# A new order of work on all engines in the time-mixing layer, reciprocals of products of two halves, crossed numerators and one first norm for two sequences on GpSimd

## The chip, the cores and the metric

One Trainium2 chip, one core of it. The metric is the device time of one execution of the kernel in microseconds (us); lower is better. The core has five engines with queues of their own, each strictly in order: TensorE (PE in the profile), VectorE (DVE), ScalarE (ACT), GpSimd (POOL) and SyncE (SP, which issues most transfers). They wait for each other by semaphores.

## The reference, cut to what matters

The model has two layers. The first is RWKV time and channel mixing followed by a routed feed-forward of eight experts, the second is linear attention followed by soft-routed experts. All is float32. The change lies in the first half of layer 0, over 16 sequences of 256 tokens with 128 features:

```python
h = ln(x, ln1); h1 = time_shift(h)                 # first norm
k, v, r = mix(h, h1) @ (Wk, Wv, Wr)
wkv = (sum_{i<t} e^{(t-1-i)w + k_i} v_i + e^{u+k_t} v_t) / (sum_{i<t} e^{(t-1-i)w + k_i} + e^{u+k_t})
x = x + (sigmoid(r) * wkv) @ Wo                    # time mixing
h = ln(x, ln2); h1 = time_shift(h)                 # second norm
x = x + sigmoid(mix(h, h1) @ cm_Wr) * (relu(mix(h, h1) @ cm_Wk)**2 @ cm_Wv)   # channel mixing
x = layernorm(x_in + x)                            # third norm; then logits = x @ router_w, top-1 expert
```

The numerator and the denominator of wkv come from one scan over time, divided per column (token) and row (feature).

## The kernel before, in words

Features lie on the 128 partitions when a stage runs along time, tokens when a norm or an output is formed. Two sequences (u = 0 and 1) make a turn; there are eight turns. Four parts of the work are pipelined over turns, and one step runs them for four different turns: **N** (first norm of turn s+2, turned to columns), **M** (time mixing of turn s+1), **C** (channel mixing of turn s), **R** (third norm's columns, router logits, places and the scatter of rows into expert order, turn s-1). Steps go from s = -2 to 8: N, NM, NMC, then NMCR in s = 1 to 5 (s = 2 to 5 are a hardware loop), MCR, CR, R. After them come a routing table, the experts and layer 1, which the change leaves as they are.

Nothing but the written order of each engine's queue and its semaphore waits sets the order of a step. The queues before:

- PE: `mixed_columns` of keys and values of both sequences (L670-675), time receptance and the turn of the second norm for each (L676-684), the turn of the third norm and the first two channel keys for each (L685-694), router logits, channel receptance `receptance` (L636) and the last two keys for each (L703-707), `time_mixing_out(0)` (L626), channel values of both (L717), turns of the first norm (L721-726), `ranks`, `time_mixing_out(1)`.
- ACT: columns of the second norm and the tanh of r for both; `shares(0)` (L755: four relus and three exponentials); the third norm of sequence 1 (`normalise`, L743-752), then columns of the third norm of both (L802); `relus` and `squares` of the keys (L776-785) around `shares(1)`; the gates (L818); the first norm of both (L822) and its columns (L826); third norm of sequence 0, second norm of both.
- DVE: `exponents` of both (a running maximum and a difference, L983), statistics of the first norm, then `weighted_values` (L1089): `take_values`, `run_state` (the scan over 512 columns, numerator and denominator), `kept_part`, `both_parts`, `inverse` (a reciprocal of the 256 denominators, L1022), `receive` (times 1 + tanh), `mixed_values` (times the reciprocal; gives `y_cols`), with the router's small steps between; then the sums and statistics of the other norms (`first_sum`, `gate_values`, `second_sum`, `stats`, `spread`).
- POOL: `to_rstd` (L867: two small operations, a power -0.5, a product) once per norm and sequence, six a step; `x01` (L929: the sum of input and first output, which also allows the next load of `x_res`); `find_places`; `scatter` (four indirect transfers).
- SP: loads of `x_in_rows` behind the first norm, of `x_res` behind `x01`, copies of the third norm to `xa` and to `stage`; the copy to `stage` waits until the scatter before has landed.

In PE's queue the turn of the third norm of a sequence comes before its first keys:

```python
for u in range(U):                                   # L685
    if "R" in parts:
        pe.wait_ge(R["normed3_ready"][u], r * NT + NT)
        turn(bank(u, 2), normed3[u], R["turned3"][u])
    if "C" in parts:
        pe.wait_ge(R["h2_ready"][u], c + 1)
        ...
```

Of the kernel before, what the change touches and what calls it, by code (L numbers as in the profile page):

```python
# [73 lines left out]
def two_layer_kernel(nc, x_in, vecs_in, rows_in, consts_in, w, out):  # L74
# [26 lines left out]
    with ctx:  # L101
# [31 lines left out]
        eps = sb("eps", [P, 3, NT])  # L133
# [75 lines left out]
        def bufs(name, shape, dt=F32, scope=rw):  # L209
# [7 lines left out]
                 for k in (1, 2, 3)}  # L217
        moments = {k: bufs(f"moments_{k}", [P, NT, 6]) for k in (1, 2, 3)}
        normed1 = bufs("normed1", [P, NT, D])
# [16 lines left out]
        recip = bufs("recip", [P, T])  # L236
# [67 lines left out]


# [243 lines left out]
        with nc.Block() as block:  # L549
# [64 lines left out]
            def _(pe):  # L614
# [10 lines left out]
                def step(parts, n, m, c, r):  # L625
                    def time_mixing_out(u):  # L626
# [20 lines left out]
                    def ranks():  # L647
                        pe.wait_ge(chosen_ready, r + 1)
                        at = T + 2 * NT * E

                        def dst(first):
                            return bank(1, 0, at + first * E, at + (TURN_TILES + 1) * E)
# [17 lines left out]
                    if "M" in parts:  # L670
                        for u in range(U):
                            pe.wait_ge(R["h1_ready"][u], m + 1)
                            mixed_columns(bank(u, 1, 0, T), h1_cols[u], "tm_Wk", 0, D)
                            mixed_columns(bank(u, 1, T, 2 * T), h1_cols[u], "tm_Wv", 0, D
                                          ).then_inc(R["kv_ready"][u], 1)
                    for u in range(U):  # L676
                        if "M" in parts:
                            if "C" in parts and follows(c):
                                pe.wait_ge(R["rc_done"][u], c)
                            mixed_columns(bank(u, 3, 0, T), h1_cols[u], "tm_Wr", 0, D  # L680
                                          ).then_inc(R["r_ready"][u], 1)
                        if "C" in parts:
                            pe.wait_ge(R["normed2_ready"][u], c * NT + NT)
                            turn(bank(u, 0), normed2[u], R["turned2"][u])
                    for u in range(U):  # L685
                        if "R" in parts:
                            pe.wait_ge(R["normed3_ready"][u], r * NT + NT)
                            turn(bank(u, 2), normed3[u], R["turned3"][u])
                        if "C" in parts:
                            pe.wait_ge(R["h2_ready"][u], c + 1)  # L690
                            if "M" in parts:
                                pe.wait_ge(R["r_done"][u], m + 1)
                            for k in (0, 1):
                                channel_keys(u, k, bank(u, 3, k * T, (k + 1) * T))
                    if "R" in parts:
                        for u in range(U):
                            pe.wait_ge(R["xa_cols_ready"][u], r + 1)
                            for j in range(NT):
                                last = pe.matmul(bank(u, 0, T + j * E, T + (j + 1) * E),
                                                 xa_cols[u][:, j * P:(j + 1) * P], router_w[:, :],  # L700
                                                 start=True, stop=True)
                            last.then_inc(R["logits_ready"][u], 1)
                    if "C" in parts:  # L703
                        for u in range(U):
                            receptance(u)
                            for k in (2, 3):
                                channel_keys(u, k, bank(u, 2, (k - 2) * T, (k - 1) * T))
# [1187 lines left out]
```

## Time and profile before

| | |
|---|---|
| median of 3 runs | 717.41 us (715.91 to 718.39) |
| the profiled execution | 714.66 us, span 713.0 us |
| busy over the span | PE 633.4 us (89%), DVE 470.3 (66%), ACT 366.8 (51%), POOL 272.0 (38%) |
| mean granted clock of TensorE | 0.957 of full speed |
| instructions | 14,924 |

The steps of layer 0 fill the first 231 us of the span, the experts and layer 1 the rest. A busy time counts instructions between their start and their end; matmul ends are modelled and overlap, so the distance between two starts says more about PE. A number in brackets in a timeline row is the engine's idle time before the instruction, and what ended it.

### The profile page before, as it was taken

The page shows a single profiled execution, that of the slowest core. Times are in us where ns is not written, and L with a number is a line of the kernel's source. Part 1 is how long each engine was busy: PE and PEld are TensorE (multiplying, and loading weights), DVE is VectorE, ACT ScalarE, POOL GpSimd, SP SyncE. Part 2 cuts the span into 40 slices and gives each one's busy share as a digit, 9 for nine tenths or more (in the row PEclk, how much of TensorE's full clock was granted, in tenths as well). Part 3 has the DMA queues.
Part 4 walks back from the last instruction along what each step waited for, and adds up shares of the span by engine and source line. Part 5 has one row for each costly group of instructions (what it writes and reads, how often), then busy time and mean ns, then how long its engine had stood idle before and what let it go on. Part 6 is the DMA issues. An engine that isn't in the chain of part 4 may idle for free.

```text
span 713.0 us, 14924 instructions
## 1 busy us (share of the span) xinstructions
PE 633.4 (89%) x4107; PEld 522.3 (73%) x4108; DVE 470.3 (66%) x1518; ACT 366.8 (51%) x818; POOL 272.0 (38%) x574
## 2 busy tenths in 40 slices
PE   4498898889875399999988999999999999999995
PEld 3387797779764299999934678777777777877773
DVE  4888888889733355545425677778777777777742
ACT  3477768777734244454401455455554555545542
POOL 2315556756365421112044333344433443332201
PEclk9699999999987599999999999999999999999998
DMA  5081111111101577777400000000000000000000
GB/s 144 15 245 54 42 48 59 59 52 37 60 31 44 184 238 253 225 244 227 125 23 12 4 5 17 16 15 15 15 15 15 15 7 8 15 16 8 8 9 15
DMA packets 39458, 46.99 MB, mean 66 GB/s; under 512 B 5184, under 2 KB 31104, under 8 KB 39424
## 3 DMA queue, kind: packets, MB, share of 16 engines
q1 hardware_dynamic: 35520, 39.50, 18.0%
q0 software_dynamic: 3328, 6.82, 3.1%
q8 instruction: 15, 0.25, 0.1%
q10 hardware_dynamic: 576, 0.26, 0.1%
q14 instruction: 19, 0.16, 0.1%
HBM read 34.58 MB, written 7.80 MB: 59 GB/s over the span
## 4 chain that ended last, share of the span: by engine, by line
PE 38%; DVE 8%; issue 2%; POOL 1%; ACT 1%; DMA 0%; DVEq 0%; POOLq 0%; ACTq 0%
PE banks L1401 8%; PE banks L1407 5%; PE banks L1523 5%; PE banks L1536 4%; PE banks L1435 4%; PE banks L1421 3%; DVE token_peak L1782 2%; PE banks L1383 2%; PE banks L1467 1%; PE banks L1501 1%; PE banks L1529 1%; PE banks L1457 1%; DVE moments_e L1690 1%; PE banks L1427 1%; DVE summed_e L1775 1%
## 5 line engine op out<-in xcount | busy, mean ns | idle before, releaser
L439 PE MATMUL banks<-xg_cols,w 128*128 128x128 f32 x624 | 77.8, 279 | 0.0
L439 PEld LDWEIGHTS banks<-xg_cols,w 128*128 128x128 f32 x624 | 74.4, 196 | 0.2 <-issue 0.2
L497 DVE SCALAR_TENSOR_TENSOR hidden<-banks,b_cols,gate 128x128 f32<-128x128 f32 x156 | 43.9, 344 | 46.4 <-ACT gate L466 46.4
L466 ACT ACTIVATE gate<-banks,b_cols 128x128 f32<-128x128 f32 x156 | 44.5, 368 | 54.9 <-PE banks L439 54.9
L1407 PE MATMUL banks<-ffn_w,act_cols 128*128 128x128 f32 x512 | 66.2, 278 | 0.7 <-ACT act_cols L1558 0.7
L1407 PEld LDWEIGHTS banks<-ffn_w,act_cols 128*128 128x128 f32 x512 | 60.6, 192 | 7.9 <-issue 6.4
L1401 PE MATMUL banks<-slots_cols,ffn_w 128*128 128x512 f32 x128 | 64.1, 606 | 0.8 <-ACT slots_cols L1573 0.8
L1558 ACT ACTIVATE act_cols<-banks 128x512 f32<-128x512 f32 x64 | 38.2, 597 | 27.3 <-PE banks L1401 27.3
L523 POOL DMA_DIRECT2D xg<-sorted_x x40 | 21.9, 547 | 79.3 <-PE banks L448 61.0
L617 PE MATMUL banks<-consts,normed 128*128 128x128 f32 x96 | 18.9, 308 | 31.7 <-ACT normed L750 31.6
L1624 POOL TENSOR_TENSOR rstd_b<-mean_var_b,eps 128x2 f32<-128x2 f32 x16 | 3.1, 195 | 106.2 <-DVE mean_var_b L1693 106.2
L871 POOL TENSOR_TENSOR rstd<-mean_var,eps 128x2 f32<-128x2 f32 x48 | 11.5, 240 | 82.7 <-DVE mean_var L981 82.5
L429 PE MATMUL banks<-w,hidden 128*128 x312 | 41.3, 275 | 0.5 <-DVE hidden L497 0.5
L622 PE MATMUL banks<-h_cols,cm_Wk_now 128*128 128x256 f32 x128 | 41.1, 405 | 0.2 <-ACT r_tanh L794 0.2
L623 PE MATMUL banks<-h_cols,cm_Wk_before 128*128 128x256 f32 x128 | 40.0, 395 | 0.0
L617 PEld LDWEIGHTS banks<-consts,normed 128*128 128x128 f32 x96 | 12.5, 155 | 37.2 <-ACT normed L750 28.4
L910 POOL DMA_INDIRECT sorted_x<-stage,slot_now x32 | 33.4, 1043 | 16.7 <-issue 12.7
L429 PEld LDWEIGHTS banks<-w,hidden 128*128 128x128 f32 x312 | 37.9, 192 | 0.7 <-issue 0.7
L1597 ACT ACTIVATE combine<-banks 128x1024 f32<-128x1024 f32 x16 | 16.4, 1023 | 40.8 <-PE banks L1529 40.8
L874 POOL TENSOR_TENSOR rstd<-rstd,neg_half 128x2 f32<-128x2 f32 x48 | 35.6, 741 | 4.0
L1613 POOL DMA_INDIRECT y_got<-sorted_y,y_idx x32 | 32.5, 1015 | 9.3 <-issue 7.5
L1523 PE MATMUL banks<-xn,dispatch 128*128 128x129 f32 x256 | 34.2, 288 | 0.2 <-ACT dispatch L1589 0.2
(242 smaller groups left out, 1628.4 us busy)
## 6 DMA issues: line engine op xcount, KB each, us to landing
w<-w_dram SPq DMA_DIRECT2D x39, 512.0 KB, 4.5
xg<-sorted_x POOLq DMA_DIRECT2D x40, 64.0 KB, 4.0
sorted_y<-y_rows SPq DMA_DIRECT2D x39, 64.0 KB, 3.4
x_in_rows<-x_dram SPq DMA_DIRECT2D x16, 128.0 KB, 2.3
x_res<-x_dram SPq DMA_DIRECT2D x16, 128.0 KB, 2.2
xa<-normed SPq DMA_DIRECT2D x16, 128.0 KB, 2.1
stage<-normed SPq DMA_DIRECT2D x16, 128.0 KB, 2.1
out_dram<-final SPq DMA_DIRECT2D x16, 128.0 KB, 1.8
```

What stands on the lines that cost most here:

```text
L429: last = pe.matmul(dst, hidden[u][:, c, :], w2[:, bass.ds(e2, 1), c, :].squeeze(1), start=(c == 0), stop=(c == XC - 1))
L439: last = pe.matmul(bank(u, k, c * P, (c + 1) * P), w1[parity][u][:, lo:lo + P], xg_cols[u][:, :], start=True, stop=True)
L466: act.activation(gate[u][:, c, :], bank(u, 2, c * P, (c + 1) * P), ACT.Sigmoid, bias=b1_cols[:, bass.ds(e1 * GC + XC + c, 1)]).then_inc(ga ...
L497: last = dve.scalar_tensor_tensor(hidden[u][:, c, :], bank(u, 1, c * P, (c + 1) * P), b1_cols[:, bass.ds(e1 * GC + c, 1)], gate[u][:, c, : ...
L622: pe.matmul(dst, now[:, lo:hi], h[:, 1:T + 1], start=True, stop=False)
L623: return pe.matmul(dst, before[:, lo:hi], h[:, 0:T], start=False, stop=True)
L874: p.step(pool.tensor_tensor(rstd[u][:, :], rstd[u][:, :], neg_half[:, 0:NT], ALU.pow))
L910: pool.indirect_dma_start(sorted_x, bass.IndirectOffsetOnAxis(ap=slot_now[:, t:t + 1], axis=0), stage[u][:, j, :], None).then_inc(scattere ...
L1401: pe.matmul(banks[:, 6 + c % 2, :], ffn_w1[:, c * P:(c + 1) * P], slots_cols[ub][:, :], start=True, stop=True).then_inc(S["hid_ready"][ub], 1)
L1407: last = pe.matmul(banks[:, 6, s * D:(s + 1) * D], act_cols[ub][:, c, s * P:(s + 1) * P], ffn_w2[:, c, :], start=(c == 0), stop=(c == HC - 1))
L1523: last = pe.matmul(dst, dispatch[uf][:, j, s * P:(s + 1) * P], xn[uf][:, j, :], start=(j == 0), stop=(j == NT - 1))
L1558: act.activation(act_cols[ub][:, c, :], banks[:, 6 + c % 2, :], ACT.Gelu).then_inc(S["gelu_ready"][ub], 1)
```

## The change

1. **Reciprocals.** The 256 denominators a sequence are split into two halves of 128. DVE multiplies the halves (`multiplied`, 128 x 128) and takes the reciprocal of the product (128 x 128 instead of 128 x 256). 1/a is then b/(ab): GpSimd multiplies each numerator by the other half's denominator (`cross`), DVE's `receive` takes that in place of the numerator, and `mixed_values` multiplies both halves by the same reciprocal.
2. **First norm.** One `norm_scales` on GpSimd for the four tiles of both sequences replaces two `to_rstd` on two tiles each; ACT's `normalise(1, ...)` of both sequences waits for it.
3. **Order.** PE, ACT, DVE and POOL get a new written order of a step. `shares` becomes `shares_taken` and `shares_kept`; `scatter` works per sequence; `find_places` stands before the third norm of sequence 1; `x01` stands behind the first half of the scatter.
4. **A new place for the ranks.** Their PSUM columns move to bank (1, 3), so `ranks` waits for the channel gate of sequence 1, and time receptance of sequence 1 waits for `places`.

```diff
@@ TensorE, one step (the functions hold the matmuls that stood in the loops)
+                    def time_receptance(u):
+                        if "C" in parts and follows(c):
+                            pe.wait_ge(R["rc_done"][u], c)
+                        if u == 1 and "R" in parts and follows(r):
+                            pe.wait_ge(places_ready, r)
+                        mixed_columns(bank(u, 3, 0, T), h1_cols[u], "tm_Wr", 0, D).then_inc(R["r_ready"][u], 1)
...
+                    def turn_first(u):
+                        pe.wait_ge(R["normed1_ready"][u], n * NT + 2 * NT)
...
                     def ranks():
                         pe.wait_ge(chosen_ready, r + 1)
+                        pe.wait_ge(R["rc_done"][1], c + 1 if "C" in parts else r + 1)
...
+                        keys_and_values(0)
+                        time_receptance(0)
+                        turn_second(0)
+                        keys_and_values(1)
+                        turn_third(0)
+                        time_receptance(1)
+                        turn_second(1)
+                        first_keys(0)
+                        token_logits(0)
+                        first_keys(1)
+                        other_keys(0)
+                        turn_third(1)
+                        receptance(0)
+                        token_logits(1)
+                        other_keys(1)
+                        channel_values(0)
+                        turn_first(0)
+                        receptance(1)
                         time_mixing_out(0)
+                        channel_values(1)
+                        time_mixing_out(1)
+                        turn_first(1)
                         ranks()
@@ ScalarE, one step
+                        second_columns(0)
+                        time_gate(0)
+                        shares_taken(0)
+                        third_columns(0)
+                        shares_kept(0)
+                        time_gate(1)
+                        second_columns(1)
+                        relus(0, 0)
+                        shares_taken(1)
                         normalise(3, r, 1, gated, normed3)
+                        shares_kept(1)
+                        third_columns(1)
                         relus(1, 0)
                         relus(0, 1)
                         squares(0, 0)
                         squares(0, 1)
+                        squares(1, 0)
                         relus(1, 1)
+                        normalise(1, n, 0, x_in_rows, normed1)
+                        channel_gate(0)
+                        normalise(1, n, 1, x_in_rows, normed1)
                         squares(1, 1)
+                        first_columns(0)
+                        channel_gate(1)
                         normalise(3, c, 0, gated, normed3)
+                        first_columns(1)
                             normalise(2, m, u, x1, normed2)
@@ GpSimd
+                    def cross(u):
+                        pool.wait_ge(vec_m, m * VALUE_STEPS + BOTH_STEP[u])
+                        p2.step(pool.tensor_tensor(in_halves(crossed[u][:, :]), in_halves(frac[u][:, 0, :]),
+                                                   in_halves(frac[u][:, 1, :])[:, ::-1, :], ALU.mult))
+                    if "M" in parts:
+                        cross(0)
                     if "N" in parts:
                         for u in range(U):
-                            to_rstd(p1, 1, EPS_TM, n, u)
+                            pool.wait_ge(R["var1"][u], n * NT + NT)
+                        norm_scales(p1, both_mean_var[:, :, :, :].rearrange("p u j k -> p (u j) k"),
...
+                        cross(1)
                         to_rstd(p3, 3, EPS_LN, c, 0)
                             to_rstd(p2, 2, EPS_TM, m, u)
+                        find_places()
                         to_rstd(p3, 3, EPS_LN, c, 1)
+                        scatter(0)
...
+                        scatter(1)
@@ VectorE
-                def inverse(q, u, both):
+                def multiplied(q, u, both):
                     q.wait(both)
-                    return q.step(dve.reciprocal(recip[u][:, :], frac[u][:, 1, :]))
+                    return q.step(dve.tensor_tensor(product[u][:, :], frac[u][:, 1, 0:T // 2],
+                                                    frac[u][:, 1, T // 2:T], ALU.mult))
+                def inverse(q, u, product_run):
+                    q.wait(product_run)
+                    return q.step(dve.reciprocal(recip[u][:, :], product[u][:, :]))
                 def receive(q, m, u):
                     dve.wait_ge(R["r_done"][u], m + 1)
+                    dve.wait_ge(pool_rwkv[2], m * (POOL_VALUES + 3 * U) + u + 1)
+                    return q.step(dve.scalar_tensor_tensor(crossed[u][:, :], r_tanh[u][:, :], 1.0,
+                                                           crossed[u][:, :], ALU.add, ALU.mult))
...
+                        highest0 = highest(qm, m, 0)
+                        exponents(qm, 0, highest0)
+                        taken0 = stats(qn, 1, x_in_rows, 0)
+                        highest1 = highest(qm, m, 1)
+                        taken1 = stats(qn, 1, x_in_rows, 1)
+                        take_values(m, 0)
+                        spread(qn, 1, 0, taken0)
+                        exponents(qm, 1, highest1)
+                        state0 = run_state(qm, m, 0)
+                        spread(qn, 1, 1, taken1)
+                        kept0 = kept_part(qm, m, 0, state0)
+                        both0 = both_parts(qm, 0, kept0)
+                        take_values(m, 1)
+                        multiplied0 = multiplied(qm, 0, both0)
+                        inverse(qm, 0, multiplied0)
+                        state1 = run_state(qm, m, 1)
+                        save_logits(qr, r)
+                        received0 = receive(qm, m, 0)
+                        best_logit(qr)
+                        kept1 = kept_part(qm, m, 1, state1)
+                        candidates(qr)
+                        both1 = both_parts(qm, 1, kept1)
+                        preferences(qr)
+                        multiplied1 = multiplied(qm, 1, both1)
+                        mixed_values(qm, 0, received0)
+                        inverse(qm, 1, multiplied1)
+                        gated0 = second_sum(qc, c, 0)
+                        received1 = receive(qm, m, 1)
+                        spread(qc, 3, 0, gated0)
+                        first_sum(qm, m, 0)
+                        mixed_values(qm, 1, received1)
+                        summed0 = first_stats(qm, m, 0)
+                        first_candidate(qr, r)
+                        spread(qm, 2, 0, summed0)
+                        choice(qr, r)
+                        first_sum(qm, m, 1)
+                        summed1 = first_stats(qm, m, 1)
                         places(r)
+                        spread(qm, 2, 1, summed1)
                         gated1 = second_sum(qc, c, 1)
                         spread(qc, 3, 1, gated1)
```

(The conditions on the parts of a step are left out of the lists of calls. `second_sum` now holds `gate_values` too.)

## Rows read from the trace of the kernel before

**Rows 1.** Busy time of each engine by step, from each step's first matmul.

```profile
core 0: us, PE busy (x) PEld busy (x) DVE busy (x) ACT busy (x) POOL busy (x), PEclk, DMA share, GB/s
9.67:31.45 21.78, 10.12 (x38) 8.29 (x37) 16.65 (x34) 9.39 (x23) 3.33 (x8) 0.73 0.19 55
31.45:53.71 22.26, 21.32 (x121) 18.11 (x120) 17.06 (x38) 15.73 (x38) 6.42 (x18) 0.96 0.70 199
53.71:77.72 24.01, 21.58 (x138) 19.01 (x138) 20.46 (x61) 18.37 (x45) 9.63 (x28) 1.00 0.14 43
77.72:102.92 25.20, 22.70 (x139) 20.32 (x138) 20.33 (x57) 18.43 (x45) 16.06 (x38) 0.93 0.17 53
126.44:149.97 23.53, 21.03 (x140) 19.08 (x138) 19.95 (x56) 18.55 (x45) 15.27 (x37) 1.00 0.18 56
173.50:202.07 28.57, 22.32 (x135) 19.81 (x134) 21.58 (x62) 18.10 (x43) 14.74 (x37) 0.92 0.13 42
```

**Rows 2.** Timeline of PE in step 4 (start, us, engine, line, operation).

```profile
136.72 0.44 PE L617 MATMUL banks<-consts,normed 128*128 128x128 f32 x2 [2.50 <-ACT normed L750]
...
145.30 3.74 PE L717 MATMUL banks<-cm_wv,k_sq 128*128 128x128 f32 x32
```

**Rows 3.** Waits from step 1 to step 6 (us in total, times, longest).

```profile
PE banks L617 <- ACT normed L750: 14.7, 6, 2.5
```

**Rows 4.** Timeline of ACT in step 4.

```profile
135.79 0.87 ACT L750 ACTIVATE normed<-gated,shift,rstd 128x128 f32<-128x128 f32 x2
...
145.55 1.14 ACT L784 ACTIVATE k_sq<-k_relu 128x512 f32<-128x512 f32 x2
146.59 0.65 ACT L818 ACTIVATE rc_tanh<-banks 128x256 f32<-128x256 f32 x2
147.12 1.64 ACT L750 ACTIVATE normed<-x_in_rows,shift,rstd 128x128 f32<-128x128 f32 x4
```

**Rows 5.** Groups of DVE instructions by line (count, busy, mean ns, idle before).

```profile
L1022 DVE RECIPROCAL recip<-frac 128x256 f32<-128x256 f32 x16 | 28.0, 1753 | 0.5
...
L1767 DVE RECIPROCAL norm_inv<-norm_inv 128x32 f32<-128x32 f32 x16 | 5.7, 354 | 0.5
...
L954 DVE TENSOR_TENSOR tm_Wk_before<-tm_Wk_before,tm_Wk_now 128x128 f32<-128x128 f32 x1 | 0.3, 293 | 0.0
```

**Rows 6.** Timeline of DVE, steps -1, 4 and 8.

```profile
18.77 0.69 DVE L997 TENSOR_TENSOR take<-take,banks 128x512 f32<-128x512 f32 x1 [1.38 <-ACT take L765]
...
141.30 1.22 DVE L1004 TENSOR_TENSOR_SCAN state<-keep_state,take 128x512 f32<-128x512 f32 x1
...
150.17 0.42 DVE L1121 TENSOR_TENSOR x<-x_res,banks 128x256 f32<-128x256 f32 x1 [0.56 <-PE banks L629]
...
151.47 0.24 DVE L981 BATCH_NORM_AGGREGATE mean_var<-moments 128x2 f32<-128x6 f32 x2
...
231.16 0.17 DVE L1086 CAST slot_now<-last_place 128x4 int32<-128x4 f32 x1 [2.61 <-DMA sorted_x<-stage,slot_now]
```

**Rows 7.** Timeline of POOL, steps 4 and 7.

```profile
130.21 0.19 POOL L871 TENSOR_TENSOR rstd<-mean_var,eps 128x2 f32<-128x2 f32 x1
...
131.60 1.42 POOL L929 TENSOR_TENSOR x<-x_res,x 128x256 f32<-128x256 f32 x2
132.99 0.24 POOL L889 TENSOR_TENSOR own_place<-place,chosen 128x32 f32<-128x32 f32 x1
...
134.48 0.18 POOL L901 COPY place_f<-own_place 128x4 f32 x1
...
139.50 0.95 POOL L910 DMA_INDIRECT sorted_x<-stage,slot_now  x1 [0.30 <-issue]
140.47 0.21 POOL L871 TENSOR_TENSOR rstd<-mean_var,eps 128x2 f32<-128x2 f32 x1
...
144.28 0.19 POOL L876 TENSOR_TENSOR shift<-shift,rstd 128x2 f32<-128x2 f32 x1
...
223.62 1.03 POOL L937 TENSOR_TENSOR slot_sq<-slot_sq,neg_half 128x4 f32<-128x4 f32 x1
```

More of the change, by code:

```diff
@@ L216, in two_layer_kernel @@
         norms = {k: (bufs(f"mean_var_{k}", [P, NT, 2]), bufs(f"rstd_{k}", [P, NT]), bufs(f"shift_{k}", [P, NT]))
-                 for k in (1, 2, 3)}
+                 for k in (2, 3)}
         moments = {k: bufs(f"moments_{k}", [P, NT, 6]) for k in (1, 2, 3)}
+        both_mean_var = sb("mean_var_1", [P, U, NT, 2], scope=rw)
+        both_rstd = sb("rstd_1", [P, U, NT], scope=rw)
+        both_shift = sb("shift_1", [P, U, NT], scope=rw)
+        norms[1] = tuple([whole[:, u] for u in range(U)] for whole in (both_mean_var, both_rstd, both_shift))
         normed1 = bufs("normed1", [P, NT, D])
@@ L235, in two_layer_kernel @@
         frac = bufs("frac", [P, 2, T])
-        recip = bufs("recip", [P, T])
+        recip = bufs("recip", [P, T // 2])
+        product = bufs("product", [P, T // 2])
+        crossed = bufs("crossed", [P, T])
+        BOTH_STEP, VALUE_STEPS, POOL_VALUES = (5, 11), 18, U
         r_tanh = bufs("r_tanh", [P, T])
@@ new lines, in first_keys, with other_keys @@
+                    def first_keys(u):
+                        pe.wait_ge(R["h2_ready"][u], c + 1)
+                        if "M" in parts:
+                            pe.wait_ge(R["r_done"][u], m + 1)
+                        elif u == 1 and "R" in parts:
+                            pe.wait_ge(places_ready, r)
+                        for k in (0, 1):
+                            channel_keys(u, k, bank(u, 3, k * T, (k + 1) * T))
+                    def other_keys(u):
+                        for k in (2, 3):
+                            channel_keys(u, k, bank(u, 2, (k - 2) * T, (k - 1) * T))
@@ new lines, in token_logits, with channel_values @@
+                    def token_logits(u):
+                        pe.wait_ge(R["xa_cols_ready"][u], r + 1)
+                        for j in range(NT):
+                            last = pe.matmul(bank(u, 0, T + j * E, T + (j + 1) * E),
+                                             xa_cols[u][:, j * P:(j + 1) * P], router_w[:, :],
+                                             start=True, stop=True)
+                        last.then_inc(R["logits_ready"][u], 1)
+                    def channel_values(u):
+                        pe.wait_ge(R["sq_ready"][u], c * 2 + 2)
+                        for j in range(NT):
+                            for k in range(HC):
+                                last = pe.matmul(bank(u, 2, j * D, (j + 1) * D),
+                                                 k_sq[u][:, k, j * P:(j + 1) * P], cm_wv[:, k, :],
+                                                 start=(k == 0), stop=(k == HC - 1))
+                        last.then_inc(R["cv_ready"][u], 1)
@@ L670, in step @@
                     if "M" in parts:
[L671 to L694, printed above, removed]
@@ L695, in step @@
-                    if "R" in parts:
[L696 to L702, printed above, removed]
@@ L939, in step @@
                     if "R" in parts:
-                        if "M" in parts:
-                            find_places()
-                        scatter()
+                        scatter(1)
                 pipeline(pool, step)
@@ L1070, in places @@
                 def places(r):
-                    at = T + 2 * NT * E
                     full = [P, TURN_TILES + 1, E]
```

293 lines of the change are left out of this document (137 added, 156 removed).

## Prediction

> **What bounds the kernel now.** I read the busy times step by step first, because the change lies in the first 231 us of a 713 us span and a share of the whole span says nothing of it. A step of the hardware loop takes 23.53 us, of which PE is busy 21.03, DVE 19.95, ACT 18.55 and POOL 15.27 [rows 1]. PE is nearest to its limit, and at full granted clock. The timeline of PE then shows that what is missing is one gap, not many: the turn of the third norm of sequence 1 waits 2.50 us for ACT [rows 2], and the stretches before and behind it are without a hole. ACT is not late because it is full but because of its order: its `normalise` of the third norm of sequence 1 starts at 135.79, right behind all of `shares(0)` [rows 4]. So the reader should see a loop bound by PE's work, about 21.0 us, plus one wait of 2.5 us that ACT's order makes. The same wait stands in steps 1 to 6 (six waits, 14.7 us in all, the longest 2.5 [rows 3]). In step 2 it also costs clock: the step reads 0.93 of full speed and 25.20 us against 23.53 [rows 1], 1.67 us; step 6 reads 0.92 and pays it too. DVE's busy time, which the reciprocals would cut, is not the bound in the loop; it is in step -1, where DVE is busy 16.65 of 21.78 us and PE 10.12 [rows 1].
>
> **The reciprocals.** A reciprocal of 256 columns takes 1753 ns and one of 32 columns 354 [rows 5]; the slope is 6.25 ns a column, so one of 128 takes 954. The new product of 128 columns has a row of its shape, 293 ns [rows 5]. DVE gains 1753 - 954 - 293 = 0.5 us a sequence, 1.0 a step. In the loop this lies beside PE's 21 us and gains nothing there; it makes room for a wait.
>
> **The crossing on POOL.** Two more operations of 128x256 a step. The nearest row is `x01`, 1.42 us for two [rows 7], so 0.74 each with start gaps; the trace has no operation that reads its halves in swapped order. **The first norm** loses two runs of 1.40 us (130.21 to 131.60) [rows 7] and gets one: the power takes 1.03 us on four columns [rows 7], with the three small operations about 1.72. POOL's own work hardly changes; what changes is who waits for it, since DVE's `receive` now waits for `cross` and ACT's whole tail for the joint norm.
>
> **The new order in the loop.** I laid the new queues against each other with the durations of step 4, PE's first keys at 0. Without a hole PE ends a step at 20.7 to 21.0. The waits behind that: keys (1) need the second norm's columns at 7.8 and start at 8.0; the third norm's turn (1), moved from the middle to 11.4, needs ACT at 10.5, so the wait of 2.5 us goes; channel values (0) need the squares at 14.4 and start at 14.7; `time_mixing_out(1)` needs y at 19.1 and starts at 19.8. Every one holds, with 0.2 to 0.9 us to spare, which is little.
>
> What is late next is POOL. Its queue from the variance of x1 of sequence 1 to the joint first norm of the next step is: `to_rstd` 1.40, `find_places` 1.67 (132.99 to 134.66), `to_rstd` 1.40, half a scatter 2.7 (0.95 and 0.30 issue, each twice, and a gap), `x01` 1.42, the other half 2.7, `cross(0)` 0.74, norm 1.72: 13.8 us [rows 7]. Then the way back to that variance: two `normalise` 1.64 with the gate 0.33 between, one of two squares 0.57 [rows 4], channel values (1), half of 3.74, about 1.8, its output matmuls 0.45 [rows 2], and DVE's sum, statistics and aggregates, about 1.2 of the stretch from 150.17 to 151.71 [rows 6], with handoffs 6.4. The ring is 13.8 + 6.4 = 20.2 us, if DVE never holds POOL up.
>
> It does: from 140.47 to 144.47 the eight small operations of the two first norms take 4.00 us [rows 7] where twice 1.40 is 2.80, while DVE runs its scan from 141.30 [rows 6] and the products behind it. The ring's `x01`, `cross(0)` and norm, 3.88 us, now stand beside the same DVE work; at the same stretch of 43% they cost 1.7 us, and the scatters up to 0.4. So the delay is 0 to 2.1, the ring 20.2 to 22.3, and the step no less than PE's 21.0. I take 1.5, nearer the upper end because it is the same DVE work: **21.7 us a loop step**. `x01` behind half a scatter releases the load of `x_res` about 3 us later, with some 6 us left before `first_sum`. The copy to `stage` on SP waits for the later half of the scatter, about 14.5 into the next step, and lands before ACT's third norm at 19.9; SP's loads of `x_in_rows` queue behind it with 2 us to spare.
>
> The Trainium skill's page "SBUF — State Buffer", section "SBUF: two separate sides", says that the port pair which DVE and GpSimd share is an exclusive lock held for a whole instruction, by a DVE operation with two SBUF inputs too. The stretch of 4.00 us agrees that POOL is held up; by a full lock on both sides the sum would be 715 us (the first rival), by the row it is 697.
>
> **The sum.** Step -1: DVE's `take_values` waits until 18.77 [rows 6] because ACT serves both gates first; the new order serves sequence 0 first, which lets it start at 16.9: 1.9 earlier. With 1.0 from the reciprocals, less 0.4 for `first_sum` ahead of the last `mixed_values` and 0.4 for a turn that is now behind `time_mixing_out(1)`: 2.1. Step 0 fills PE's holes, 22.26 - 21.32: 0.9. Step 1: its POOL ring has no scatter before it, so PE's holes go too, 24.01 - 21.58 [rows 1]: 2.4. Steps 2 to 5: 25.20 + 3 x 23.53 - 4 x 21.7 = 9.0. Step 6 ends with the turn of the next step's second norm, 28.57 us [rows 1]; it loses the wait of 2.5, the slow clock's 1.7, and about 2.0 because `first_sum(0)` no longer queues behind both sequences' values: 22.3, so 6.2. Steps 7 and 8: `ranks` now stands in front of channel values (1) and waits for the gate, 0.5 later, and the slots' norm stands inside the scatter, whose landing DVE awaits for 2.61 us anyway [rows 6]: -0.5. In all 2.1 + 0.9 + 2.4 + 9.0 + 6.2 - 0.5 = 20.1. Against the profiled execution's own 714.66 us (span 713.0 and 1.7 around it) that is 694.6; that execution lies 2.75 below the median of the runs, 717.41, so the forecast for the median is **697.3 us**. From the routing table on all moves as it stands.
>
> **Rivals.**
> *A full lock.* If POOL and DVE shut each other out for whole instructions, the ring grows by all of DVE's two-input SBUF time from `x01` to the norm: two scans of 1.22, four products of 0.69, a small product and one `receive`, 5.9 us. The step is then 26.1 and the four loop steps lose 8.6 where I gain 9.0: gain 20.1 - 17.6 = 2.5, about 715 us. For it: the 4.00 us. Against it: DVE's scan beside POOL takes 1.22 [rows 6] as the others do, and POOL's eight operations took 43% longer, not twice as long. Chance 0.05.
> *The PE wait only moves.* The margins of 0.2 to 0.9 are used up by handoffs, ACT's order or a late `receive`, and a step stays at 22.5 to 23.5. At 23.0 the loop gains 25.20 + 70.59 - 92.0 = 3.8 instead of 9.0, and step 1 about 1.5 less: 13.4 in all, about 704 us; with nothing gained in any PE wait but the clock and the two ends, 709. For it: ACT's list from the second norm's columns to the last squares has 14.8 us of work in one piece. Against it: PE has no other wait before. Chance 0.19.
> *A slow crossing (slower than before).* No row shows POOL reading two halves in swapped order. POOL's whole round of a step is 13.8 + 0.74 + 2.8 = 17.3 us with the crossing at 0.74. The kernel loses once a loop step takes more than (95.8 + 20.1 - 9.0) / 4 = 26.7 us, so once a crossing takes 5.4 us, seven times the row. At 8 us it is 31.8 a step and about 738 us. Against it: `find_places`, five small operations on strided views, fits in 1.67 us [rows 7]. Chance 0.05.
> *No gain, as the reciprocals are not the bound.* True of the reciprocals alone: 717, if the order did nothing. Chance 0.03.
>
> **The numbers.** Forecast 0.68: steps of 21.0 to 22.3, with about 1 us either way from the ends, 693.5 to 701. Range 690 to 706: it takes in the nearer half of the second rival, and at its lower end a loop at PE's limit with ends that gain 4 us more. About 0.3%, 2 us, is what a measurement can tell from no change. Faster 0.90 (the forecast, the moved wait and half of the lock), within it 0.05, slower 0.05.
>
> **What would show it.** Right: PE starts a loop step every 21.0 to 22.3 us; the wait of the third norm's turn is gone; granted clock 1.00 in steps 1 to 5; `recip` at 0.95 and `product` at 0.29 us; the first PE wait left is for `normed1` or for squares, behind POOL's norm. Wrong: `crossed` over 2 us, DVE waiting for it over 1 us a step, or a PE wait of 2 us at any turn.

## The result, and the profile after

| | before | after |
|---|---|---|
| median of 4 runs | 717.03 us (715.91 to 718.39) | 708.10 us (706.20 to 709.14) |
| profiled execution, its span | 714.66, 713.0 us | 706.20, 704.5 us |
| ratio | | 0.9874, 95% interval 0.9856 to 0.9893 |

The kernel is 8.9 us faster. The forecast was 697.3 with a range of 690 to 706: the sign was right, the gain came to less than half, and the time lies above the range. By the two profiled executions, against which the sum was made, 8.5 us came and 20.1 were forecast.

Busy times of the kernel after by step (steps -1 to 6 from each step's first matmul; the last row runs from the turn of step 7's second norm to the first expert matmul):

```profile
core 0: us, PE busy (x) PEld busy (x) DVE busy (x) ACT busy (x) POOL busy (x), PEclk, DMA share, GB/s
9.67:29.48 19.81, 9.72 (x36) 7.79 (x37) 16.00 (x39) 9.38 (x22) 4.14 (x9) 0.72 0.21 62
29.48:50.36 20.88, 20.88 (x121) 18.55 (x121) 16.95 (x45) 16.35 (x38) 8.32 (x17) 0.94 0.69 217
50.36:72.05 21.69, 21.05 (x139) 19.00 (x138) 19.50 (x58) 18.22 (x44) 10.99 (x27) 1.00 0.16 50
72.05:95.50 23.45, 21.43 (x143) 19.23 (x139) 21.08 (x60) 18.88 (x46) 18.11 (x38) 1.00 0.18 57
118.31:141.36 23.05, 21.33 (x139) 19.28 (x138) 20.61 (x59) 18.35 (x45) 17.51 (x35) 1.00 0.18 57
164.30:189.53 25.23, 21.34 (x139) 18.90 (x136) 22.23 (x60) 17.91 (x43) 17.04 (x36) 0.99 0.14 46
189.53:233.57 44.04, 21.85 (x123) 18.27 (x124) 13.06 (x56) 12.94 (x34) 23.83 (x46) 0.69 0.25 81
```

Against [rows 1], with the forecast in brackets: step -1 gains 1.97 us (2.1), step 0 1.38 (0.9), step 1 2.32 (2.4), steps 2 to 5 together 3.5 (9.0; they take 92.25 us, 23.06 each, where 21.7 was forecast), step 6 3.3 (6.2). Steps 7 and 8 with the routing lose 2.1 (41.90 us before, from 202.07 to the first expert matmul at 243.97; forecast -0.5), and the experts and layer 1 lose 1.9 (469.0 us before, 470.9 after; 0). So the fill (steps -1 to 1) is right, to about 1 us: in e10 below, whose code is the same up to step 7, step -1 takes 20.43 us and step 2 starts at 73.00. Four pieces are not: the loop is 5.5 short, step 6 2.9, the tail 1.6, the rest 1.9.

What ended the waits of the loop (four turns; us in total, times, longest):

```profile
ACT normed L800 <- POOL shift L957: 19.8, 13, 2.2
...
PE banks L627 <- ACT normed L800: 6.2, 4, 1.6
...
DVE crossed L1122 <- POOL crossed L995: 1.6, 4, 0.4
```

The 2.5 us for the third norm [rows 3] are gone and the granted clock is 1.00. The four waits of 1.55 us that PE has left are for the turn of the first norm of sequence 0, and ACT, which makes it, waits for POOL. POOL's queue in step 3 shows why (from the variance of x1, at 96.27, to the joint first norm):

```profile
96.35 0.19 POOL L952 TENSOR_TENSOR rstd<-mean_var,eps 128x2 f32<-128x2 f32 x1 [0.18 <-DVE mean_var L1072]
...
101.71 1.09 POOL L989 DMA_INDIRECT sorted_x<-stage,slot_now  x1 [0.73 <-issue]
...
104.55 1.42 POOL L1022 TENSOR_TENSOR x<-x_res,x 128x256 f32<-128x256 f32 x2
106.14 1.25 POOL L989 DMA_INDIRECT sorted_x<-stage,slot_now  x1 [0.17 <-issue]
...
108.69 1.69 POOL L995 TENSOR_TENSOR crossed<-frac 128x256 f32<-128x256 f32 x1
110.34 0.19 POOL L952 TENSOR_TENSOR rstd<-mean_var,eps 128x4 f32<-128x4 f32 x1
110.50 0.41 POOL L953 TENSOR_SCALAR shift<-mean_var 128x4 f32<-128x4 f32 x1
111.00 1.43 POOL L955 TENSOR_TENSOR rstd<-rstd,neg_half 128x4 f32<-128x4 f32 x1
112.51 0.47 POOL L957 TENSOR_TENSOR shift<-shift,rstd 128x4 f32<-128x4 f32 x1
112.93 0.72 POOL L995 TENSOR_TENSOR crossed<-frac 128x256 f32<-128x256 f32 x1
```

The ring that the prediction named is there (a chain that starts again in each step: POOL's queue from one variance to the joint norm, and the way back over ACT, PE and DVE to the next). From 96.35 to 112.98 it takes 16.63 us, the 13.8 that the prediction listed and a delay of 2.8. The way back, from there to the next such variance at 119.37, takes 6.4 as forecast; together 23.0, the step. DVE at the same time:

```profile
104.53 2.00 DVE L1108 TENSOR_TENSOR frac<-frac,take 128x512 f32<-128x512 f32 x1
...
107.37 0.95 DVE L1117 RECIPROCAL recip<-product 128x128 f32<-128x128 f32 x1
108.24 1.62 DVE L1094 TENSOR_TENSOR_SCAN state<-keep_state,take 128x512 f32<-128x512 f32 x1
...
110.41 0.42 DVE L1122 SCALAR_TENSOR_TENSOR crossed<-r_tanh,crossed 128x256 f32<-128x256 f32 x1 [0.41 <-POOL crossed L995]
111.56 0.69 DVE L1108 TENSOR_TENSOR frac<-frac,take 128x512 f32<-128x512 f32 x1
...
119.12 0.25 DVE L1072 BATCH_NORM_AGGREGATE mean_var<-moments 128x2 f32<-128x6 f32 x2
```

The engines hold each other up both ways. `both_parts(0)` takes 2.00 us where that of sequence 1 takes 0.69: POOL's two `x01`, 1.42 us together, stand beside it. The second scan takes 1.62 instead of 1.23, and the crossing, started 0.45 us into it, 1.69 instead of 0.72. (The scan also starts while the last transfer of the scatter is issued; e2 shows that this is not what lengthens it.)

### The profile page after: what moved, and what is told of

Read it like the earlier page. It is cut to its first block and busy times, and to the rows that moved or that the text cites. A ratio compares the mean times of both kernels' runs of the same rounds, so it can differ in the third digit from the quotient of the medians.

```text
span 704.5 us, 14982 instructions
## 1 busy us (share of the span) xinstructions
PE 630.2 (89%) x4107; PEld 521.4 (74%) x4108; DVE 471.4 (67%) x1534; ACT 366.8 (52%) x818; POOL 284.2 (40%) x558
## 5 line engine op out<-in xcount | busy, mean ns | idle before, releaser
L627 PE MATMUL banks<-consts,normed 128*128 128x128 f32 x96 | 20.6, 301 | 28.2 <-ACT normed L800 28.2
L989 POOL DMA_INDIRECT sorted_x<-stage,slot_now x32 | 35.5, 1108 | 15.6 <-issue 11.5
L955 POOL TENSOR_TENSOR rstd<-rstd,neg_half 128x2 f32<-128x2 f32 (+1 forms) x40 | 33.2, 829 | 3.3
L1636 PE MATMUL banks<-processed,combine 128*128 128x129 f32 x256 | 32.8, 281 | 0.8 <-DVE processed L1898 0.8
```

The lines of the kernel that those rows point to most:

```text
L989: pool.indirect_dma_start(sorted_x, bass.IndirectOffsetOnAxis(ap=slot_now[:, t:t + 1], axis=0), stage[u][:, j, :], None).then_inc(scattere ...
L1636: last = pe.matmul(banks[:, 7, j * N129:(j + 1) * N129], combine[ub][:, s, j * P:(j + 1) * P], processed[ub][:, s, :], start=(s == 0), sto ...
```

## Experiments

The step in a table is the mean of the three between the first matmuls of steps 3 and 6; "tail" runs from the start of step 6 to the first expert matmul. Times are medians, ratios those to the kernel before, which ran again beside each (medians of 716.1 to 717.6 us).

| kernel | time, us | ratio, interval | start of step 2 | step | tail |
|---|---|---|---|---|---|
| before | 717.03 | | 77.72 | 23.52 | 70.47 |
| after | 708.10 | 0.9874, 0.9856-0.9893 | 72.05 | 22.93 | 69.27 |
| e1 norm first | 712.11 | 0.9915, 0.9883-0.9946 | 73.03 | 24.22 | 68.56 |
| e2 cross on DVE | 706.46 | 0.9822, 0.9773-0.9871 | 75.41 | 22.07 | 68.86 |
| e3 no crossing | 706.10 | 0.9819, 0.9772-0.9866 | 74.71 | 22.31 | 68.64 |
| e4 crossing alone | 728.25 | 1.0127, 1.0078-1.0175 | 81.18 | 26.20 | 71.27 |
| e5 sum late | 712.03 | 0.9937, 0.9916-0.9957 | 79.86 | 22.04 | 69.18 |
| e6 + tail | 706.94 | 0.9876, 0.9849-0.9904 | 79.88 | 22.07 | 66.42 |
| e7 late in the loop | 702.11 | 0.9774, 0.9735-0.9812 | 73.37 | 22.04 | 67.17 |
| e8 e7, no crossing | 702.62 | 0.9780, 0.9746-0.9814 | 74.88 | 22.39 | 66.39 |
| e9 two norms | 706.57 | 0.9857, 0.9832-0.9882 | 72.31 | 23.02 | 68.96 |
| e10 tail alone | 705.28 | 0.9843, 0.9814-0.9873 | 73.00 | 22.94 | 67.35 |
| e11 e7, step 6 | 701.90 | 0.9794, 0.9763-0.9825 | 73.53 | 22.05 | 66.96 |

**e1: the norm ahead of the crossing.**

```diff
-                    if "M" in parts:
-                        cross(0)
                     if "N" in parts:
                         ...
+                    if "M" in parts:
+                        cross(0)
```

> Only the joint first norm and the first crossed numerator change places on GpSimd, so the norm no longer waits behind the crossing. Theory A (the loop step is set by GpSimd's ring from the second norm to the joint first norm, 16.6 us, plus the way back of 6.4): the norm is done about 1.6 us earlier in a step, TensorE's wait of 1.54 us for the first norm goes, the step comes from 23.06 to 21.5 to 22.4 us (the crossing then comes late to VectorE by about 1 us, which takes part of it back), the whole 702 to 706 us. Rival B (VectorE's wait for the crossed numerators is what holds the step): the wait of 0.41 us a step for the first one grows to 1.2 to 2 us, the step stays at 23 us or grows, and the whole is 708 us or more.

B held. Waits of its loop, as above:

```profile
DVE crossed L1122 <- POOL crossed L995: 8.2, 4, 2.2
...
PE banks L696 <- DVE y_cols L1127: 6.6, 7, 1.3
```

The wait for the norm is gone, and what replaced it is larger: DVE waits 2.05 us a step for `crossed`, so PE waits for `y_cols`. The crossing and the norm serve two paths with hardly any slack, and only one can be first on POOL.

**e2, e3: the crossing off POOL.** e2 makes both crossed products on VectorE, e3 goes back to reciprocals over 256 columns in the new order:

```diff
 e2, in receive():
-                    dve.wait_ge(pool_rwkv[2], m * (POOL_VALUES + 3 * U) + u + 1)
+                    q.wait(q.step(dve.tensor_tensor(in_halves(crossed[u][:, :]), in_halves(frac[u][:, 0, :]),
+                                                    in_halves(frac[u][:, 1, :])[:, ::-1, :], ALU.mult)))
 e3, in inverse():
-                    return q.step(dve.reciprocal(recip[u][:, :], product[u][:, :]))
+                    return q.step(dve.reciprocal(recip[u][:, :], frac[u][:, 1, :]))
```

> The two crossed products of a step are made on VectorE instead of GpSimd; everything else is as in the changed kernel. Theory A: GpSimd's ring loses 1.65 us and the longer power that ran beside the scan (0.4), VectorE has 0.84 us more work and loses its wait of 0.41 and the scan's 0.39 of lengthening: step 21.4 to 22.2 us, whole 701 to 705 us. Rival B (VectorE is as close to the bound as GpSimd): step 23.0 us or more, whole 708 us or more.

> The changed kernel's order on all engines with the old reciprocals over 256 columns, and no product and no crossing. Theory A (the order gives the whole gain; the crossing only lengthens GpSimd's ring): reciprocals 1.75 instead of 0.95 + 0.29 us, VectorE 0.5 us a sequence more, GpSimd's ring 2 us shorter: step 21.6 to 22.6 us, whole 702 to 706 us. Rival R (the shorter reciprocals carry the gain): step 23.6 us or more, whole 711 us or more.

Both steps shrink by 0.6 to 0.9 us, as A said, though the reciprocal of e3 takes 1.74 us again. Both start step 2 later by 2.7 to 3.4 us (about 1 us of which can be spread, by e10): in the fill DVE sets the end, and there the shorter DVE work counts. For this both miss A's range for the whole, e2 by 1.5 us and e3 by 0.1. The order carries the gain of the loop, the crossing takes some of it back. In e2 the second scan starts in the issue of the last transfer as in the kernel after, and is not lengthened:

```profile
110.56 0.96 POOL L989 DMA_INDIRECT sorted_x<-stage,slot_now  x1 [0.30 <-issue]
...
111.10 1.16 DVE L1085 TENSOR_TENSOR_SCAN state<-keep_state,take 128x512 f32<-128x512 f32 x1
...
111.54 0.71 POOL L952 TENSOR_TENSOR rstd<-mean_var,eps 128x4 f32<-128x4 f32 x1
```

**e4: the crossing in the old order.** The kernel before with `product`, half-width `recip` and two `cross` behind POOL's two first norms.

```diff
                     if "N" in parts:
                         for u in range(U):
                             to_rstd(p1, 1, EPS_TM, n, u)
+                    if "M" in parts:
+                        for u in range(U):
+                            cross(u)
```

> The kernel before, in its old order, with the reciprocals of products and the crossing on GpSimd alone (after the two first norms). Theory A: TensorE's waits there are for the third norm of sequence 1 and for the first norm, which this does not shorten: 715 to 719 us, a step 23.3 to 24.0 us. Rival R (the reciprocals carry the gain): VectorE 1 us a step shorter, 707 to 712 us.

Both were wrong: it is slower by 1.27%. From its waits:

```profile
DVE crossed L1047 <- POOL crossed L923: 10.4, 3, 4.0
```

The crossing stands behind all four scatters and both first norms, DVE waits up to 4.0 us for it, and 1.0 us a step of shorter reciprocals buys nothing.

**e5: the sum `x01` behind the joint norm.** From between the two scatters of a step to the next step, where the same turn is the one of channel mixing.

```diff
-                    if "M" in parts:
-                        for u in range(U):
-                            pool.wait_ge(R["x1_ready"][u], m + 1)
...
+                    if "C" in parts:
+                        for u in range(U):
+                            pool.wait_ge(R["x1_ready"][u], c + 1)
...
```

> The sum x01 (two operations on GpSimd, 1.42 us) is moved from between the two scatters of a step to behind the joint first norm of the next step; nothing else. Theory A with the lock (the sum stretches VectorE's addition both_parts(0) from 0.69 to 2.00 us, and stands in GpSimd's ring ahead of crossing and norm): both_parts(0) takes 0.7 us, the first crossing 0.7 to 0.9 us, the joint norm is done about 2.5 us earlier in a step, TensorE's wait for the first norm (1.55 us) is gone, the step comes from 23.06 to 21.6 to 22.0 us, the whole to 699 to 703 us. Rival (the lock is off the path, and TensorE only waits for something else): step 22.6 us or more, whole 706 us or more.

In the loop it came as A said: `both_parts(0)` takes 0.69 us, the crossing, which now starts 0.15 us ahead of the scan, 0.74, PE's wait for the first norm is gone, the step is 22.04. (The joint norm still takes 3.1 us, now beside the scan.) The step alone doesn't show what the hold-up was worth: the sum's own 1.42 us left the ring too, and 16.63 - 1.42 + 6.4 = 21.6 us lies below 22.04 already. The whole is 9 us above A's range and slower than after, because steps 0 and 1 lost 7.2 us. Its SP queue and DVE in the fill:

```profile
45.19 1.50 SPq L588 DMA_DIRECT2D x_res<-x_dram  x2
...
49.48 6.62 SPq L611 DMA_DIRECT2D w_qkv<-W_qkv_dram  x1
...
58.68 0.94 SPq L581 DMA_DIRECT2D x_in_rows<-x_dram  x2
```

```profile
62.38 0.49 DVE L1066 BATCH_NORM_STATS2 moments<-x_in_rows 128x6 f32<-128x128 f32 x2 [6.04 <-DMA x_in_rows<-x_dram]
```

The load of `x_res` waits for `x01`, and behind it in SP's queue stand the weights and the next input. In the kernel after the three rows start at 32.88, 36.72 and 46.97.

**e6, e7: the tail, and the sum late only in the loop.** e6 adds to e5 a new order for step 7 alone: `ranks` before `channel_values(0)` in the bank that the kernel before used, so that they don't wait for the gate; `find_places` ahead of the third norm of sequence 0, `scatter(0)` ahead of that of sequence 1. e7 keeps this, and leaves `x01` (`sums`) in its own step for the first two turns:

```diff
+                    if parts in ("NM", "NMC"):
+                        sums(m)
...
-                    if "C" in parts:
+                    if "C" in parts and parts != "NMC" and not (isinstance(n, int) and n == 3):
```

> As e5, and in the last step with channel mixing the ranks are made before the channel values (in the place in the banks that the kernel before used, so that they do not wait for the gate), the places are found ahead of the third norm of sequence 0, and the first scatter stands ahead of the third norm of sequence 1. Theory T (the tail lost 1.7 us because the ranks wait for the gate of sequence 1 and the slots' norm stands behind a scatter): from the first turn of step 7 to the first expert matmul 41.5 to 43 us instead of 44.04, the whole 1 to 2.5 us less than e5. Rival (the tail is set by the scatters' transfers and by the logits of the last turn): 44 us as before, the whole as e5.

> As e6, but the sum x01 stays in its own step for the first two turns and goes behind the joint first norm only from the third on, so that the load of x_res that waits for it on SyncE's queue no longer holds up the loads of the weights and of the next input rows behind it. Theory A with the queue: the fill steps are again those of the changed kernel (step 2 begins at 72 to 73 us instead of 79.9), the loop steps stay at 22.1 to 22.2 us (TensorE is busy all but 1 us of them), the tail stays 2.5 us shorter: span 697 to 699, whole 698.5 to 702 us. Rival (the lost 6 us of e5 and e6 come from the sum itself in the first steps): whole 705 us or more.

e6 shortens the tail by 2.8 us (of its 5.1 us less than e5, 2.3 lie in the experts and layer 1, where nothing changed), and e7 brings the fill back to 73.37. T held for the tail; the whole of e6 came further below e5 than the 1 to 2.5 us expected, by those 2.3. A of e7 held, with the start of step 2 0.4 us and the whole 0.1 us above their ranges. Steps 3, 4 and 6 of e7:

```profile
96.16:118.27 22.11, 21.39 (x137) 19.19 (x138) 20.25 (x59) 17.98 (x44) 16.93 (x35) 1.00 0.18 58
118.27:140.45 22.18, 21.40 (x138) 19.21 (x138) 20.38 (x59) 18.33 (x45) 17.12 (x35) 1.00 0.19 59
...
162.28:186.98 24.70, 21.36 (x136) 18.92 (x134) 21.54 (x60) 18.02 (x43) 17.26 (x36) 1.00 0.15 47
```

PE is busy all but 0.7 to 0.8 us of a loop step, and its longest wait there is 0.4.

**e8: e7 with the old reciprocals**, as e3 does it.

> As e7 with the old reciprocals over 256 columns, no product and no crossing (the chain of VectorE as in e3). Theory A (in the loop the crossing gives nothing once TensorE is the bound; it only shortens the fill, where VectorE sets the end): fill 2 to 2.7 us longer than in e7, loop steps 22.0 to 22.4 us, whole 1.5 to 4 us more than e7. Rival R (the shorter reciprocals are worth something in the loop too): loop steps 22.8 us or more and the whole 6 us or more above e7. Rival S (the crossing is of no use at all): the same as e7 or less.

The fill is 1.5 us longer, and a step 0.35: 22.39 where the four kernels with crossing and the late sum (e5, e6, e7, e11) lie between 22.04 and 22.07. So in this order the shorter reciprocals are worth a little in the loop too, which no theory had. In the whole it doesn't show: what lies behind step 6, where the code is the same, reads 1.1 us less than in e7, and the medians lie 0.5 us apart, within their intervals. A's 1.5 to 4 us did not come, and S is not ruled out for the whole.

**e9: two first norms.** The joint norm is `to_rstd` for each sequence again.

> The changed kernel with the joint first norm taken apart again: two norms over 2 columns each (1.4 us each by the rows of the second norm) in the same place behind the first crossing, in place of one over 4 columns that takes 2.64 us there. Theory A (TensorE waits for the first norm of sequence 0 alone, and the joint one makes it wait for that of sequence 1): sequence 0 is done about 1.2 us earlier in a step, the wait of 1.55 us shrinks to 0.5 us or less, step 21.9 to 22.4 us instead of 23.06, whole 702.5 to 705.5 us. Rival J (one joint norm saves GpSimd time on the ring, so two cost it): step 23.0 us or more, whole 708 us or more.

A fell, and of J the step held but not the whole. PE's wait fell to 1.0 us, but the squares of sequence 1, behind that sequence's later norm in ACT's queue, gave 0.4 back; the step is the same, and the joint norm is worth nothing either way:

```profile
PE banks L627 <- ACT normed L800: 3.9, 4, 1.0
...
PE banks L688 <- ACT k_sq L861: 1.6, 4, 0.4
```

**e10: the tail of e6 on the kernel after.**

> The changed kernel with the order of the last step with channel mixing of e6 alone (ranks before the channel values, places and first scatter ahead of the third norms); loop and fill as in the changed kernel. Theory T: from the start of step 6 to the first expert matmul 66.4 to 67.2 us as in e6 and e7 instead of 69.27, the whole 705 to 707 us. Rival (the gain of e6 in the tail came with its later sum): 69 us, the whole 708 us.

It held within 0.2 us: the tail is 1.9 us shorter and the loop the same (22.94).

**e11: step 6.** In step 6 alone, `second_sum(0)` goes behind `choice` on VectorE, and the second norm of sequence 0 ahead of the third on GpSimd and ScalarE.

> As e7, but in step 6 alone (the last with time mixing) the first residual sum of sequence 0 goes ahead of the second one on VectorE, and its second norm ahead of the third norm on GpSimd and on ScalarE. Theory S (step 6 ends 2.5 us later than forecast because first_sum(0) queues behind second_sum(0) on VectorE): the turn of the second norm of sequence 0, 24.70 us after the step's start in e7, comes at 22.5 to 23.5, the first keys of step 7, which also need sequence 1's turn, 0.5 to 1.3 us earlier, the whole 700.5 to 702 us. Rival L (the chain's own latencies or sequence 1 set it): first keys not earlier than in e7 by more than 0.3 us.

The turn of sequence 0 came 23.22 us into the step, as S said, but the first keys of step 7 came at 26.71 (26.76 in e7): they stand behind the turn of sequence 1, which was no earlier. Rival L held by its number. The reason lies in the edit: in e11 `second_sum(0)` and its statistics stand ahead of the first sum of sequence 1, whose matmuls end at 183.31.

```profile
182.70 0.61 PE L699 MATMUL banks<-wo,y_cols 128*128 128x128 f32 x4
...
182.90 0.42 DVE L1220 SCALAR_TENSOR_TENSOR gated<-rc_tanh,banks 128x256 f32<-128x256 f32 x1
...
184.69 0.42 DVE L1210 TENSOR_TENSOR x<-x_res,banks 128x256 f32<-128x256 f32 x1
```

That sum starts 22.24 us into the step; in e7 it starts at 21.99. An order with both first sums ahead was not run.

## Why the prediction was half right

**The sign, the place and the mechanism were right.** The wait for the third norm went with the clock loss of step 2, the next bound is POOL's ring, `recip` takes 0.95 and `product` 0.28 to 0.29 us, and step -1, where DVE sets the end, gains 1.97 of 2.1 (1.35 in e10). None of the prediction's signs of being wrong appeared in the loop either: the longest crossing takes 1.70 us, DVE waits 0.41 us a step for it, PE at most 1.6 at a turn.

**The step that failed is "so the delay is 0 to 2.1 ... I take 1.5", and with it 21.7 us a loop step.** The delay is 2.8, above the upper bound: 0.92 on the joint norm (2.64 for 1.72), 0.95 on the first crossing (1.69 for 0.74), 0.85 on the first half of the scatter (from 100.99 to 104.54, 3.55 for 2.7), the rest in small pieces.

The scatter's part was a wrong row. The prediction took both halves from the last two transfers of step 4; the first two took 3.2 to 3.8 us in steps 2 to 6 of the kernel before, with 0.86 of issue ahead (135.52, step 4) and a longer second transfer in some (113.41, step 3):

```profile
113.41 1.48 POOL L910 DMA_INDIRECT sorted_x<-stage,slot_now  x1 [0.30 <-issue]
...
135.52 1.09 POOL L910 DMA_INDIRECT sorted_x<-stage,slot_now  x1 [0.86 <-issue]
```

In e5, without `x01` between the halves, it takes 3.57. The other two parts are hold-ups, and the bound scaled them by the 43% that POOL's small operations showed in step 4. What the rows show is that an operation of one engine can wait for all that is left of the other's. Step 3 of the kernel before has it, where an operation of 0.22 us takes as long as the scan that it meets:

```profile
117.71 1.23 POOL L872 TENSOR_SCALAR shift<-mean_var 128x2 f32<-128x2 f32 x1
...
117.71 1.22 DVE L1004 TENSOR_TENSOR_SCAN state<-keep_state,take 128x512 f32<-128x512 f32 x1
```

The edits show it for the long ones: `both_parts(0)` takes 2.00 to 2.02 us in the loop of every kernel that has `x01` beside it (after, e2, e3, e9) and 0.69 where it is moved (e5, e7); the crossing takes 1.69 from 0.45 us into the scan and 0.74 from 0.15 us ahead of it, where the scan takes 1.65 to 1.68 (e5, e7). The Trainium skill's page "SBUF — State Buffer", section "SBUF: two separate sides", says this as an exclusive lock; the trace agrees with that more than the prediction did (0.69 + 1.42 is 2.11, `both_parts` took 2.00), but not with the Trainium skill's rule there that the instruction which starts first gets the lock: by the rows the addition starts 0.02 us ahead, and is held. The rival of the full lock was not right either: it charged all 5.9 us of DVE's two-input work, and only what meets in time counts.

**The floor was too low as well.** "No less than PE's 21.0": with the ring relieved a step takes 22.04 (e5, e7), since PE's busy time is 21.4 in the new order and small waits add 0.7. So 21.7 was out of reach even without the delay. Over steps 2 to 5, the four that were forecast, e5 and e7 take 22.23 us a step; so of the 1.36 us that a step is over 21.7, about 0.5 are this and 0.8 the ring.

**The rival "the PE wait only moves"** had the time (704 to 709 us) and, in part, the way: steps of 22.5 to 23.5, the wait now at the first norm. ACT's list was not the cause; ACT itself waits for POOL.

**Step 6** (6.2 forecast, 3.3 come) was costed to the turn of sequence 0 as if that ended it, with "about 2.0 because `first_sum(0)` no longer queues". It still queues: its matmuls end at 183.46 and it starts at 185.28, behind `second_sum(0)` and what follows that. e11 takes it out of there, and that turn comes 1.5 us earlier and the next keys not at all, for the reason given under e11. The ring's delay has only a small share: without it (e5, e7) the step to that turn is still 24.7.

**The tail** was given 0.5 and lost 2.1. The slots' norm behind a scatter was said to cost nothing, as DVE awaits a landing anyway. In the kernel after:

```profile
206.12 0.18 PE L721 MATMUL banks<-chosen,upper_bf 128*128 128x40 bf16 x1 [0.56 <-ACT rc_tanh L850]
```

```profile
216.31 1.14 DVE L1307 SCALAR_TENSOR_TENSOR slot_rows<-slot_rows,slot_sq,rows 128x128 f32<-128x128 f32 x4 [6.05 <-POOL slot_sq L1030]
...
220.27 0.17 DVE L1182 CAST slot_now<-last_place 128x4 int32<-128x4 f32 x1 [0.49 <-DMA sorted_x<-stage,slot_now]
```

```profile
217.92 0.99 POOL L989 DMA_INDIRECT sorted_x<-stage,slot_now  x1 [0.30 <-issue]
```

DVE's wait for the landing shrank from 2.61 [rows 6] to 0.49, so DVE is late too, but the landing still comes last, and it is itself late: the last transfer of that scatter ends 29.4 us after the first turn of step 7, where it ended after 27.7 in the kernel before (at 229.79, from 202.07). Of these 1.7 us, 1.15 are there when the variance of sequence 1 is ready (after 20.73 us, 19.58 before), and PE's wait of 0.56 for the gate, shown above, is part of them. The other 0.5 come up in POOL's queue from there on, where the slots' norm stands between the halves of the scatter, and 0.5 more behind the scatter. e10 ends that transfer after 27.7 again and gets 1.9 back by order alone.

**Experts and layer 1**, at 0, read 1.9 more. Their code is the same in all thirteen profiles, which read 469.0 (before, the lowest) to 472.1 us (e2). That is the spread of this part, and no effect of the change can be told from it.

**The reciprocals**, named for no gain in the loop, give none in the kernel after, where a step is 0.6 us shorter without them and their crossing (e3); once the ring is out of the way they give 0.35 a step (e8), which the whole doesn't show. That the crossing would cost in its place was in the prediction only as a wait that fits. In the old order it costs 11 us (e4).

## What to carry to other kernels

When an operation moves from VectorE to GpSimd, price it by what it will stand beside in time: it can wait for all that is left of the other engine's operation, or the other for it (here an addition 1.3 us for two sums of 1.42 together, a crossing 1.0 for a scan). Take a cost from the place in the queue where the operation will stand: here the first half of a scatter took 3.2 to 3.8 us and the row taken gave 2.7. Before moving an operation, list the loads whose release it gives and what stands behind them in the issuing queue: in e5 a sum worth 0.9 us a step cost 7 us in the fill. And ask of each shortened operation whether its engine sets the end there: here it did in the fill, and in the loop only by 0.35 us a step after the ring was relieved.

## What the runs showed of the hardware that was not expected

- VectorE's addition of 128x512 was held from 0.69 to 2.00 us by GpSimd's two sums, though its row starts 0.02 us ahead of theirs (104.53 and 104.55), and its row ends 0.56 us after that of the second.
- A small GpSimd operation that starts beside a scan ends with it: in e7 the first operation of the joint norm took 1.14 us instead of 0.19, from 108.62 to 109.76, beside a scan of 1.68 that ends at 109.78; in e2 it took 0.71 beside a scan of 1.16 (rows above).
- The scan's lengthening goes with the crossing on GpSimd, not with the issue of an indirect transfer: it takes 1.62 us where it starts in the last transfer and a crossing follows (after), 1.16 where it starts there and none follows (e2). Where scan and crossing start together, in step 6 of e7, the scan takes 1.23 and the crossing 1.74.
- In e1 VectorE's wait for `crossed` grew from 0.41 to 2.05 us a step, with a norm of 2.3 to 2.6 us ahead of it. At the end of its step 2 PE waited 1.31, 0.76 and 0.42 us, and the granted clock of the next 4.2 us was 0.60 (97.78 to 102.00); that step took 24.80 us.
